# Row numbers and edge weights read from PSUM on VectorE, gather offsets taken directly, and a rearranged seam, in a two-layer graph kernel

## The chip, the cores and the metric

The kernel runs as one program on one NeuronCore of a Trainium2 chip. The metric is the device time of that core in microseconds (us). Before the change it is 3225.76 us, the median of three runs (3219.61 to 3226.62). The engines are called PE (TensorE), PEld (its weight loads), DVE (VectorE), ACT (ScalarE), POOL (GpSimd) and SP (SyncE).

## The reference, cut to what matters

The input is a graph of N = 6250 nodes with 128 features and E = 106,250 edges, sorted by destination. Two attention layers follow each other; both sum over the edges that end in a node:

```python
# layer 0, 8 heads of 16
q_dst = Q[dst] + rel_q[edge_type]
k_src = K[src] + rel_k[edge_type] + time_emb @ Wt + bt
v_src = V[src] + rel_v[edge_type]
logits = alpha * sum(q_dst * k_src) / 4 * decay + (1 - alpha) * hyp(m[src], m[dst]) * decay
ex = exp(logits - segment_max(logits, dst)[dst])
attn = ex / segment_sum(ex, dst)[dst]
agg = segment_sum(v_src * attn, dst)      # then Wo, residual, layer norm, FFN, layer norm
# layer 1, 4 heads of 32: the same scheme
logits = sum(leaky_relu(xs[src] + xd[dst] + edge_emb[edge_type]) * att)
agg = segment_sum(xs[src] * softmax(logits over dst), dst)   # then gate, W_out, residual, norms
```

## The kernel before, in words

Nodes are cut into blocks of 120. Edges are worked on in steps of 128; a step lies within one tile of 128 edges and one block, so that a tile with edges of two blocks gives two steps. Four steps make a quad (QS = 4), and there are 221 quads. The program's stages run behind each other: `front` (schedule, projections and tables), `edges0` (the first pass over all edges), `join_tiles` and `nodes0`, `edges1` (the second pass), `join_tiles` and `nodes1`.

Both passes have the same plan. Each engine runs its own list, written out by hand in a function `emit(None, c)` that is called for one iteration c after the other; semaphores tie the lists together. For each quad:

- POOL issues four indirect DMAs (`gather`, L1087 and L1823), which bring 128 rows each from a table in DRAM into a ring in SBUF, `rows`. The ring holds 12 quads in the first pass (RQ0) and 16 in the second (RQ). The row numbers that steer a gather, its offsets, are copied by ACT from a large index tensor into a small tile `idx` ahead of time (`index`, L1217 and L1927), and POOL waits for that copy once in a group. Before a slot is used again, POOL waits for `sums` of the quad that had it.
- `node`, one node number for each edge, comes by DMA from SP. From it a transposed one-hot `oht` is made: on DVE in the first pass (`transposed_onehot`, L1110) and with two ACT instructions in the second (L1934, L1943).
- PE (`edge`, L1290 and L1997) adds up in PSUM (`p_x`) the gathered rows and, through `oht`, the rows of the destinations.
- DVE makes the logits from that, in the first pass by L1146 (plus time features), L1151 (times the queries) and L1156 (sum by head), in the second by L1860, L1869 and L1879.
- After a group of quads (LQ0 = 4 in the first pass, LQ = 8 in the second) comes the seam: PE transposes the group's logits into PSUM (`p_l`), DVE takes running maxima over each node's edges with two scans, ACT takes the exponential, PE transposes back into PSUM (`p_e`), and ACT copies the weights beside the gathered rows (L1243, L1957; semaphore `spread`).
- Some quads later (LAG0 = 7 and LAG = 10) the same quad is summed. DVE builds the one-hot `oh`, 128x(4x122), by comparing the row numbers 0 to 121 (`k.iota`) with `k.code` (L1164, L1865), and multiplies the gathered values with the weights that lie beside them (L1180, L1876; `scaled`). PE multiplies `oh` with the weighted rows into `p_r` (L1320, L2033; `sums`), ACT evicts `p_r` to `bound`, and DVE adds its four steps to the accumulator (`add`, L1135 and L1889).

The block that a step belongs to is known only on the chip. DVE reads it into registers with `load_steps` and uses it as the address of the accumulator, sixteen steps at a time:

```python
if live(i, a) and (a % 4 == 3 or a == 0):
    count["blocks"] = load_steps(nc, k, ET.DVE, 1, nth0(i, a, QS), 4 if a % 4 == 3 else 3)
```

In the first pass this is the first thing in DVE's iteration (L1125), ahead of L1146 and behind a wait for the last add of the iteration before. In the second it stands behind L1879 (L1891).

The second pass starts behind `nodes0` and a clearing of semaphores. There SP loads the index tensor `index1` (L1794), ACT copies the first offsets (L1932), and DVE zeroes the two accumulators with memsets of 120x7128 (L1846) and scales the attention row (L1848).

Of the kernel before, what the change touches and what calls it, by code (L numbers as in the profile page):

```python
# [26 lines left out]
P = 128  # L27
# [99 lines left out]
class Kept:  # L127


    def __init__(self, nc, ctx, io, sz):  # L130
# [29 lines left out]
        self.pair = sb("pair", [P, RQ0 * QS * R0])  # L160
        self.tops = sb("tops", [P, S // (LQ0 * QS), 2])
# [799 lines left out]
def edges0(nc, k):  # L961
# [7 lines left out]
    with ExitStack() as ctx:  # L969
# [7 lines left out]
        idx = [sb(f"idx{u}", [P, GS], I32) for u in range(3)]  # L977
# [17 lines left out]
        p_l, p_e = p_le[:, 0:P], p_le[:, 2 * P:3 * P]  # L995

        weights_in, ready, idx_in = sem("weights_in"), sem("ready"), sem("idx_in")
# [9 lines left out]
        vec = sem("vec")  # L1007
# [16 lines left out]
        with nc.Block() as block:  # L1024
# [78 lines left out]
            def _(dve):  # L1103
                V = nc.vector
                v = Chain(dve, vec)
                V.memset(wbd[:, :, :], 0.0).then_inc(ready, 1)
                v.did(V.memset(acc, 0.0))
# [12 lines left out]
                def emit(i, c):  # L1120
# [4 lines left out]
                    if live(i, a) and (a % 4 == 3 or a == 0):  # L1125
                        count["blocks"] = load_steps(nc, k, ET.DVE, 1, nth0(i, a, QS), 4 if a % 4 == 3 else 3)

                    def add(t):
# [4 lines left out]
                        to = acc[:, bass.ds(count["blocks"][((a - 3) % 4 if a >= 3 else a) * QS + t], 1), :]  # L1133
# [36 lines left out]
                    if maxing:  # L1170
                        u = m1 // LQ0 % 3
                        dve.wait_ge(turned, group(i, m1, 1, 1))
                        dve.wait_ge(group_in[u], slot(i, m1, RQ0, 16 * 2))
                        v.did(V.tensor_tensor(scaled_l[:, :], p_l, decay[u][:, :], ALU.mult))
                    if live(i, w):
                        if w % LQ0 == 0:
                            dve.wait_ge(spread, group(i, w, 1, 1))
                        r = w % RQ0 * QS
# [21 lines left out]
                    if live(i, a):  # L1200
                        dve.wait_ge(vec, count["added"])
                        dve.sem_inc(added, 1)
# [1294 lines left out]
```

## Time and profile before

| | before |
|---|---|
| median of three runs | 3225.76 us (3219.61 to 3226.62) |
| the profiled execution, its own time | 3207.44 us |
| its span, first to last instruction | 3205.6 us |
| mean granted TensorE clock | 0.889 of full speed |
| PE busy | 2423.5 us (76%) |
| DVE busy | 2361.2 us (74%) |
| POOL busy | 1935.5 us (60%) |
| ACT busy | 1398.0 us (44%) |

The profile shows one execution with every instruction's start and duration. "Busy" leaves out waits, register work and DMA issues on all engines but POOL, whose indirect DMAs count as its work. A group is all instructions of one line, operation and shape; behind the bar stand their busy time, the mean of one, and the idle time of the engine just before them with what ended it. "Issue" is idle time that no wait of the profile explains. The first gather of the first pass starts at 315.75 us, that of the second at 1876.48.

### The profile page before, as it was taken

How to read it: one execution, taken by the hardware profiler on the slowest of the kernel's cores; microseconds unless marked ns; L12 is line 12 of the kernel's file. 1: busy time of each engine (PE TensorE's matmuls, PEld its weight loads, DVE VectorE, ACT ScalarE, POOL GpSimd, SP SyncE). 2: the span in 40 equal slices, each digit the busy share in tenths (PEclk: the TensorE clock that was granted, in tenths of full speed). 3: DMA queues.
4: the chain of work that ended last, by engine and by line, in shares of the span. 5: the costliest groups of instructions: out<-in, count | busy, mean ns of one | idle time of the engine just before them, and what ended most of it. 6: DMA issues, size and time to landing. Idle time of an engine off the chain costs nothing. (4 is left out here: it accounts for less than half of the span.)

```text
span 3205.6 us, 48812 instructions
## 1 busy us (share of the span) xinstructions
PE 2423.5 (76%) x11946; PEld 1882.5 (59%) x11946; DVE 2361.2 (74%) x5743; ACT 1398.0 (44%) x4327; POOL 1935.5 (60%) x1957
## 2 busy tenths in 40 slices
PE   4887789888888888887578846767677677666744
PEld 3565566666666666666333435666666666666633
DVE  7444798988898888988656646667666766666767
ACT  2433355555555555554155533333333333333306
POOL 1000777777777777774600047777777777777464
PEclk8898899999999999998799978888888888888865
DMA  5376766666666666673200133333333333333131
GB/s 112 58 208 199 209 196 196 195 193 194 195 194 194 191 192 195 194 194 98 67 16 25 32 89 72 79 83 83 82 83 83 82 83 83 82 82 82 36 61 41
DMA packets 253628, 387.14 MB, mean 121 GB/s; under 512 B 70853, under 2 KB 168881, under 8 KB 249642
## 3 DMA queue, kind: packets, MB, share of 16 engines
q0 software_dynamic: 86432, 239.62, 28.7%
q1 hardware_dynamic: 132662, 130.96, 16.1%
q10 hardware_dynamic: 34260, 13.43, 1.7%
q8 instruction: 107, 1.75, 0.2%
q14 instruction: 167, 1.37, 0.1%
HBM read 342.88 MB, written 40.92 MB: 120 GB/s over the span
## 5 line engine op out<-in xcount | busy, mean ns | idle before, releaser
L1831 POOL DMA_INDIRECT pair<-d_table,e_idx x884 | 868.1, 982 | 563.6 <-ACT e_idx L1932 294.6
L1094 POOL DMA_INDIRECT pair<-d_table,e_idx x884 | 899.7, 1018 | 276.6 <-issue 248.2
L2007 PE MATMUL e_p_x<-pair,iden 128*128 128x264 f32 x884 | 343.7, 476 | 318.7 <-issue 250.2
L1308 PE MATMUL e_p_x<-big,e_oht 128*128 x1768 | 455.4, 380 | 0.0
L1966 ACT COPY pair<-e_p_r 122x264 f32<-122x264 f32 x442 | 165.5, 375 | 633.8 <-PE e_p_r L2033 632.0
L1860 DVE SCALAR_TENSOR_TENSOR e_prod<-e_p_x,e_att 128x512 f32<-128x512 f32 x221 | 152.9, 692 | 315.0 <-PE e_p_x L2009 302.6
L2007 PEld LDWEIGHTS e_p_x<-pair,iden 128*128 128x128 f32 x884 | 158.6, 223 | 352.6 <-issue 319.2
L1308 PEld LDWEIGHTS e_p_x<-big,e_oht 128*128 128x128 f32 x1768 | 337.4, 191 | 46.4
L2009 PEld LDWEIGHTS e_p_x<-big,e_oht 128*128 128x128 f32 x1768 | 335.3, 234 | 46.5
L1298 PE MATMUL e_p_t<-e_wbd,e_feat 128*128 128x512 f32 x442 | 243.6, 633 | 144.6 <-DVE pair L1146 117.5
L2009 PE MATMUL e_p_x<-big,e_oht 128*128 x1768 | 335.1, 322 | 0.0
L1260 ACT ACTIVATE e_p_x<-e_p_x 128x128 f32<-128x128 f32 x884 | 234.2, 265 | 179.3 <-DVE pair L1151 178.7
L2033 PE MATMUL e_p_r<-pair,e_oh 128*122 128x132 f32 x1768 | 270.1, 301 | 52.3 <-DVE pair L1876 49.2
L2033 PEld LDWEIGHTS e_p_r<-pair,e_oh 128*122 128x122 f32 x1768 | 246.2, 208 | 68.4 <-DVE pair L1876 67.5
L1135 DVE TENSOR_TENSOR big<-big,e_bound 120x136 f32 x884 | 257.2, 291 | 22.7 <-DVE e_lg L1183 15.0
L1306 PE MATMUL e_p_x<-pair,iden 128*128 128x256 f32 x884 | 264.3, 381 | 0.0
L1320 PE MATMUL e_p_r<-pair,e_oh 128*122 128x136 f32 x1768 | 252.7, 287 | 7.5 <-DVE pair L1180 7.5
L1320 PEld LDWEIGHTS e_p_r<-pair,e_oh 128*122 128x122 f32 x1768 | 228.0, 189 | 28.6 <-DVE pair L1180 21.5
L1306 PEld LDWEIGHTS e_p_x<-pair,iden 128*128 128x128 f32 x884 | 168.8, 191 | 118.4 <-issue 106.8
L1889 DVE TENSOR_TENSOR big<-big,pair 120x132 f32 x884 | 210.7, 291 | 30.0 <-issue 18.7
L1252 ACT COPY e_bound<-e_p_r 122x272 f32<-122x272 f32 x442 | 164.6, 385 | 140.2 <-PE e_p_r L1320 83.0
L1146 DVE TENSOR_TENSOR pair<-pair,e_p_t 128x512 f32<-128x512 f32 x221 | 151.5, 685 | 97.6 <-issue 72.6
(362 smaller groups left out, 4223.7 us busy)
## 6 DMA issues: line engine op xcount, KB each, us to landing
pair<-d_table,e_idx POOLq DMA_INDIRECT x1768, 3.5
e_node<-d_node SPq DMA_DIRECT2D x28, 960.0 KB
e_node<-d_node SPq DMA_DIRECT2D x111, 240.0 KB
d_table<-tab_kmv SPq DMA_DIRECT2D x54, 360.0 KB, 3.5
e_feat<-in_edge_attr ACTq DMA_DIRECT2D x442, 16.0 KB
e_feat<-in_edge_attr SPq DMA_DIRECT2D x442, 16.0 KB
e_gate<-d_gate SPq DMA_DIRECT2D x84, 64.5 KB
d_decay<-pair SPq DMA_DIRECT2D x7, 512.0 KB, 4.5
```

The costliest lines, as they stand in the source:

```text
L1094: nc.gpsimd.indirect_dma_start(rows[:, c % RQ0 * QS + t, 0:3 * D], None, k.d_table0, bass.IndirectOffsetOnAxis(ap=idx[c // LQ0 % 3][:, c % ...
L1135: v.did(V.tensor_tensor(to, to, bound[a // BQ % 3][0:BN, a % BQ * QS + t, :].unsqueeze(1), ALU.add))
L1260: last = A.activation(p_x[c % 2][:, t, D:2 * D], p_x[c % 2][:, t, D:2 * D], ACT.Square, accum_out=d2[c // LQ0 % 3][:, c % LQ0 * QS + t:c % ...
L1298: M(p_t[:, :, :].rearrange("p t d -> p (t d)"), feat[c % 6][:, :], wbd[:, :, :].rearrange("p t d -> p (t d)"), start=True, stop=True).then ...
L1306: M(x[:, 2 * h:2 * h + 2, D:2 * D], k.iden[:, :], rows[:, r + 2 * h:r + 2 * h + 2, D:2 * D], start=True, stop=True)
L1308: last = M(x[:, t, :], oht[c % 3][:, t * P:(t + 1) * P], qm[:, bass.ds(of[t], 1), :], start=False, stop=True, skip_group_check=True)
L1320: last = M(p_r[h][0:R_LAST + 1, t - 2 * h, 0:W], oh[w % 2][:, t, :], rows[:, w % RQ0 * QS + t, 2 * D:R0], start=True, stop=True)
L1831: nc.gpsimd.indirect_dma_start(rows[:, r, :], None, k.d_table1, bass.IndirectOffsetOnAxis(ap=idx[c // LQ % 2][:, c % LQ * QS + t:c % LQ * ...
L1889: v.did(V.tensor_tensor(to, to, bound[a // 4 % 2][0:BN, a % 4 * QS + t, :].unsqueeze(1), ALU.add))
L2007: M(x[:, 2 * h:2 * h + 2, 0:W], k.iden[:, :], rows[:, r + 2 * h:r + 2 * h + 2, :], start=True, stop=False)
L2009: last = M(x[:, t, 0:W], oht[c % 4][:, t * P:(t + 1) * P], xd[:, bass.ds(held["blocks"][(c - 1) % 4 * QS + t if c else t], 1), :], start=F ...
L2033: last = M(p_r[h][0:R_LAST + 1, t - 2 * h, 0:W], oh[w % 2][:, t, :], rows[:, w % RQ * QS + t, :], start=True, stop=True)
```

## The change

- Both passes: the row numbers 0 to 121 are copied once into a free part of a PSUM bank (`p_iota`), and the build of `oh` reads them there. The weights for the multiplication are read from the transposed exponentials in PSUM (`p_e`) instead of from beside the rows. The copy of the weights beside the rows, which the sums need, is made by DVE instead of ACT.
- Since PE writes transposes into the bank that DVE reads, DVE waits for the transposes (`turned`, `back`) before it builds `oh`; PE issues them behind its wait for `scaled`, and in the second pass the first transpose of a seam ahead of `edge(c + 1)`.
- The gathers take their offsets straight from `index0` and `index1`; the `idx` tiles, ACT's copies and POOL's waits for them are gone. `index1` lies at the end of `pair` and is loaded by SP at the start of `nodes0`.
- First pass: DVE loads four block numbers in each quad, behind the build of `oh`, for the quad after. Two small vectors (`unpart`, `ones`) are made and not used; the transposed one-hots stay on DVE.
- Second pass: the accumulators are zeroed by two ACT instructions behind its first one-hots; DVE's first iteration waits for them.

```diff
@@ Kept
+        self.index1 = self.pair[:, RQ0 * QS * R0 - S:RQ0 * QS * R0].bitcast(I32)
@@ edges0
-        p_l, p_e = p_le[:, 0:P], p_le[:, 2 * P:3 * P]
+        p_l, p_iota = p_le[:, 0:P], p_le[:, P:P + R_LAST + 1]
+        p_e = p_le[:, 2 * P:3 * P]
...
-                    if c % LQ0 == 0:
-                        pl.wait_ge(idx_in, group(i, c, 1, 1))
...
-                            bass.IndirectOffsetOnAxis(ap=idx[c // LQ0 % 3][:, c % LQ0 * QS + t:c % LQ0 * QS + t + 1], axis=0))\
+                            bass.IndirectOffsetOnAxis(ap=k.index0[:, c * QS + t:c * QS + t + 1], axis=0))\
...
+                v(V.tensor_copy(p_iota, k.iota[:, 0:R_LAST + 1]))
...
-                    if live(i, a) and (a % 4 == 3 or a == 0):
-                        count["blocks"] = load_steps(nc, k, ET.DVE, 1, nth0(i, a, QS), 4 if a % 4 == 3 else 3)
...
-                        to = acc[:, bass.ds(count["blocks"][((a - 3) % 4 if a >= 3 else a) * QS + t], 1), :]
+                        to = acc[:, bass.ds(count["blocks"][t], 1), :]
...
+                    if maxing:
+                        dve.wait_ge(turned, group(i, m1, 1, 1))
                     if live(i, w):
+                        if w % LQ0 == 0:
+                            dve.wait_ge(back, group(i, w, 1, 1))
                         if i is not None or w >= 2:
                             dve.wait_ge(sums, nth0(i, w - 1, 2))
-                        V.tensor_tensor(oh[w % 2][:, :, :], bc(k.iota[:, 0:R_LAST + 1], 1, QS),
+                        V.tensor_tensor(oh[w % 2][:, :, :], bc(p_iota, 1, QS),
                                         bc(k.code[:, bass.ds(nth0(i, w, QS), QS)], 2, R_LAST + 1), ALU.is_equal)
+                    if live(i, a + 1):
+                        upcoming = load_steps(nc, k, ET.DVE, 1, nth0(i, a + 1, QS), 1)
...
-                            dve.wait_ge(spread, group(i, w, 1, 1))
-                        r = w % RQ0 * QS
+                            V.tensor_copy(rows[:, r:r + GS, 3 * D:R0], p_e.rearrange("p (h t) -> p t h", h=H0)).then_inc(spread, 1)
...
-                        V.tensor_tensor(val, val, bc(rows[:, r:r + QS, 3 * D:R0], 3, D // H0), ALU.mult).then_inc(scaled, 1)
+                        share = p_e.rearrange("p (h t) -> p t h", h=H0)[:, w % LQ0 * QS:w % LQ0 * QS + QS, :]
+                        V.tensor_tensor(val, val, bc(share, 3, D // H0), ALU.mult).then_inc(scaled, 1)
...
-                    if c % LQ0 == 3 and live(i, m1):
-                        act.wait_ge(back, group(i, m1, 1, 1))
-                        r = m1 % RQ0 * QS
-                        A.copy(rows[:, r:r + GS, 3 * D:R0], p_e.rearrange("p (h t) -> p t h", h=H0)).then_inc(spread, 1)
...
                         pe.wait_ge(scaled, nth0(i, w + 1))
+                    if c % LQ0 == 1 and live(i, c - 1 - LQ0):
+                        g = c - 1 - LQ0
+                        pe.wait_ge(leveled, group(i, g, 1, 1))
+                        nc.tensor.transpose(p_l, lg[g // LQ0 % 3][:, :, :].rearrange("p h t -> p (h t)"), k.iden[:, :])\
+                            .then_inc(turned, 1)
+                    if c % LQ0 == 3 and live(i, c - 3 - LQ0):
+                        g = c - 3 - LQ0
+                        pe.wait_ge(exps, group(i, g, 1, 1))
+                        nc.tensor.transpose(p_e, ext[:, :], k.iden[:, :]).then_inc(back, 1)
+                    if live(i, w):
+                        if w % LQ0 == 0:
+                            pe.wait_ge(spread, group(i, w, 1, 1))
...
-                    if c % LQ0 == 0 and live(i, c - LQ0):
...
-                    if c % LQ0 == 2 and live(i, c - 2 - LQ0):
...
@@ nodes0
+                sp.dma_start(k.index1, k.d_index1).then_inc(index_in, 16)
                 sp.wait_ge(folded, 1)
@@ edges1
-                sp.dma_start(index1[:, :], k.d_index1).then_inc(index_in, 16)
...
-                for u in range(2):
-                    v.did(V.memset(k.acc1[u], 0.0))
+                v(V.tensor_copy(p_iota, k.iota[:, 0:R_LAST + 1]))
...
+                    if maxing:
+                        dve.wait_ge(turned, m // LQ + 1 if i is None else i * 2 + (m // LQ + 1))
...
-                        V.tensor_tensor(oh[w % 2][:, :, :], bc(k.iota[:, 0:R_LAST + 1], 1, QS),
+                        V.tensor_tensor(oh[w % 2][:, :, :], bc(p_iota, 1, QS),
...
-                            dve.wait_ge(spread, w // LQ + 1 if i is None else i * 2 + (w // LQ + 1))
+                            dve.wait_ge(back, w // LQ + 1 if i is None else i * 2 + (w // LQ + 1))
...
+                dve.wait_ge(zeroed, 2)
                 whole(emit)
...
-                act.wait_ge(index_in, 16)
-                index(None, 0)
                 act.wait_ge(signs, 2)
                 for c in range(3):
                     distance(None, c)
                     transposed_onehot(None, c)
+                for u in range(2):
+                    A.activation(k.acc1[u], k.part[0:BN, 0:1].unsqueeze(2).broadcast_to([BN, NBP, W]), ACT.Copy, scale=0.0)\
+                        .then_inc(zeroed, 1)
...
-                    if live(i, c + 1):
-                        edge(i, c + 1)
                     if c % LQ == 0 and live(i, m):
                         pe.wait_ge(x_read, nth(i, m + LQ) if live(i, m + LQ - 1) else sz.quads)
                         nc.tensor.transpose(p_l[:, :], lg[m // LQ % 2][:, :, :].rearrange("p h t -> p (h t)"), k.iden[:, :])\
                             .then_inc(turned, 1)
+                    if live(i, c + 1):
+                        edge(i, c + 1)
+                    if live(i, w):
+                        pe.wait_ge(scaled, nth(i, w + 1))
```

## Rows read from the trace of the kernel before

**Rows 1.** Windows of both passes: us, busy us (x) by engine, PEclk, DMA share, GB/s.
```profile
400.00:1440.00 1040.00, 929.81 (x4421) 714.11 (x4420) 934.00 (x2260) 558.21 (x2307) 800.83 (x785) 1.00 0.69 194
1960.00:2980.00 1020.00, 718.81 (x4036) 632.41 (x4036) 711.86 (x1872) 399.93 (x900) 777.13 (x798) 0.84 0.37 82
```

**Rows 2.** The page's groups: POOL's gathers of both passes.
```profile
L1831 POOL DMA_INDIRECT pair<-d_table,e_idx x884 | 868.1, 982 | 563.6 <-ACT e_idx L1932 294.6
L1094 POOL DMA_INDIRECT pair<-d_table,e_idx x884 | 899.7, 1018 | 276.6 <-issue 248.2
```

**Rows 3.** Timeline, first pass, POOL: start, us, engine, line, operation [idle before].
```profile
601.44 1.70 POOL L1094 DMA_INDIRECT pair<-d_table,e_idx  x1 [0.30 <-issue]
603.45 0.95 POOL L1094 DMA_INDIRECT pair<-d_table,e_idx  x1 [0.30 <-issue]
...
622.58 1.70 POOL L1094 DMA_INDIRECT pair<-d_table,e_idx  x1 [0.30 <-issue]
```

**Rows 4.** The same stretch on DVE.
```profile
600.85 0.66 DVE L1164 TENSOR_TENSOR e_oh<-iota_f,code 128x488 f32<-128x488 f32 x1
601.42 0.69 DVE L1180 TENSOR_TENSOR pair<-pair 128x512 f32<-128x512 f32 x1
602.02 0.30 DVE L1135 TENSOR_TENSOR big<-big,e_bound 120x136 f32 x1
```

**Rows 5.** DVE's waits: us in total, times, longest.
```profile
DVE e_prod L1860 <- PE e_p_x L2009: 302.6, 109, 8.8
DVE pair L1146 <- issue: 72.6, 54, 1.4
...
DVE pair L1146 <- DVE big L1135: 24.3, 105, 0.6
```

**Rows 6.** DVE's groups by form: busy us, mean ns, idle us before.
```profile
L1135 DVE TENSOR_TENSOR big<-big,e_bound 120x136 f32 x884 | 257.2, 291 | 22.7 <-DVE e_lg L1183 15.0 <-DVE big L1135 4.8 <-issue 2.9
...
L1180 DVE TENSOR_TENSOR pair<-pair 128x512 f32<-128x512 f32 x221 | 150.3, 680 | 0.0
L1151 DVE TENSOR_TENSOR pair<-pair,e_p_x 128x512 f32<-128x512 f32 x221 | 150.3, 680 | 7.8 <-PE e_p_x L1308 7.7
...
L1174 DVE TENSOR_TENSOR e_scaled_l<-e_p_le,e_decay 128x128 f32<-128x128 f32 x56 | 15.8, 282 | 0.0
```

**Rows 7.** Timeline, second pass, DVE, at a load of sixteen block numbers.
```profile
2282.01 0.17 DVE L1879 TENSOR_TENSOR e_lg<-e_lg,e_p_x 128x16 f32<-128x16 f32 x1
2282.88 0.95 DVE L1889 TENSOR_TENSOR big<-big,pair 120x132 f32 x4 [0.69 <-issue]
```

**Rows 8.** Timeline of all engines, the second pass's start.
```profile
1872.16 0.34 SPq L1794 DMA_DIRECT2D pair<-d_index  x1
...
1875.44 0.22 ACT L1932 COPY e_idx<-pair 128x32 int32<-128x32 int32 x1 [7.04 <-DMA pair<-d_index]
...
1876.48 1.04 POOL L1831 DMA_INDIRECT pair<-d_table,e_idx  x1 [294.58 <-ACT e_idx L1932]
...
1880.32 7.80 POOL L1831 DMA_INDIRECT pair<-d_table,e_idx  x1 [0.31 <-issue]
...
1883.90 0.72 ACT L1941 ACTIVATE e_oht<-e_node,e_unpart 128x512 f32<-128x512 bf16 x1 [8.25 <-DMA e_node<-d_type]
...
1887.15 0.16 DVE L1848 TENSOR_SCALAR e_att<-e_att 128x128 f32<-128x128 f32 x1
```

**Rows 9.** Timeline, second pass, DVE and POOL.
```profile
2218.45 0.94 POOL L1831 DMA_INDIRECT pair<-d_table,e_idx  x1 [0.30 <-issue]
...
2218.84 0.69 DVE L1860 SCALAR_TENSOR_TENSOR e_prod<-e_p_x,e_att 128x512 f32<-128x512 f32 x1 [7.35 <-PE e_p_x L2009]
...
2219.45 0.66 DVE L1865 TENSOR_TENSOR e_oh<-iota_f,code 128x488 f32<-128x488 f32 x1
...
2219.70 1.22 POOL L1831 DMA_INDIRECT pair<-d_table,e_idx  x1 [0.31 <-issue]
...
2222.39 0.69 DVE L1860 SCALAR_TENSOR_TENSOR e_prod<-e_p_x,e_att 128x512 f32<-128x512 f32 x1
```

More of the change, by code:

```diff
@@ L1105, in _ @@
                 v = Chain(dve, vec)
+                V.tensor_scalar(unpart[:, :], k.part[:, :], -1.0, None, ALU.mult).then_inc(signs, 1)
+                V.memset(ones[:, :], 1.0).then_inc(signs, 1)
                 V.memset(wbd[:, :, :], 0.0).then_inc(ready, 1)
+                v(V.tensor_copy(p_iota, k.iota[:, 0:R_LAST + 1]))
                 v.did(V.memset(acc, 0.0))
@@ L1202, in emit @@
                         dve.sem_inc(added, 1)
+                    if live(i, a + 1):
+                        count["blocks"] = upcoming
                     count["base"] += v.n
@@ L1215, in _ @@
                 A = nc.scalar
-                def index(i, c):
-                    if i is not None or c >= 3 * LQ0:
-                        b = c - 2 * LQ0 - 1
-                        act.wait_ge(rows_in[b % RQ0], slot(i, b, RQ0, 16 * QS))
-                    A.copy(idx[c // LQ0 % 3][:, :], k.index0[:, bass.ds(nth0(i, c, QS), GS)]).then_inc(idx_in, 1)
                 tiles = {}
@@ L1236, in emit @@
                 def emit(i, c):
[L1237 to L1243 removed]
+                    w = c - LAG0 - 1
                     if live(i, w):
@@ L1276, in emit @@
                         A.copy(k.tops[:, bass.ds(group(i, g), 1), :], top[g // LQ0 % 2][:, 0:P:P - 1].unsqueeze(1)).then_inc(kept, 1)
-                for g in range(2):
-                    index(None, g * LQ0)
                 for c in range(5):
@@ L1755, in edges1 @@
         att = sb("att", [P, D])
-        idx = [sb(f"idx{u}", [P, LQ * QS], I32) for u in range(2)]
         oht = [sb(f"oht{u}", [P, QS * P]) for u in range(4)]
@@ L1861, in emit @@
                                                      ALU.max, ALU.mult))
+                    m = c - LQ
+                    maxing = c % LQ == 0 and live(i, m)
+                    if maxing:
+                        dve.wait_ge(turned, m // LQ + 1 if i is None else i * 2 + (m // LQ + 1))
                     if live(i, w):
@@ L1892, in emit @@
                         counted["blocks"] = load_steps(nc, k, ET.DVE, 1, nth(i, a, QS), 4 if a else 1)
-                    m = c - LQ
-                    maxing = c % LQ == 0 and live(i, m)
                     if maxing:
@@ L1925, in _ @@
                 A = nc.scalar
-                def index(i, c):
-                    u = c // LQ % 2
-                    if i is not None or c >= 2 * LQ:
-                        b = c - LQ - 1
-                        act.wait_ge(rows_in[b % RQ], 16 * QS * (b // RQ + 1) if i is None else i * (16 * QS) + 16 * QS * (b // RQ + 1))
-                    A.copy(idx[u][:, :], index1[:, bass.ds(nth(i, c, QS), LQ * QS)]).then_inc(idx_in, 1)
                 def distance(i, c):
@@ L1950, in emit @@
                         distance(i, c + 3)
-                    if c % LQ == 2 and live(i, c - 2 + LQ):
-                        index(i, c - 2 + LQ)
-                    if c % LQ == 1 and live(i, c - 1 - LQ):
-                        m = c - 1 - LQ
-                        act.wait_ge(back, m // LQ + 1 if i is None else i * 2 + (m // LQ + 1))
-                        r0 = m % RQ * QS
-                        A.copy(rows[:, r0:r0 + LQ * QS, D:W], p_e[:, :].rearrange("p (h t) -> p t h", h=H1)).then_inc(spread, 1)
                     if live(i, w):
```

50 lines of the change are left out of this document (20 added, 30 removed).

## The prediction

> **What bounds the kernel now.** I read the busy time of the two gather passes, then POOL's groups, then POOL and DVE side by side in a few microseconds of each pass, then DVE's waits. In both passes POOL is busy for 77% of the time and no engine for 100% [rows 1], but the 884 gathers of a pass stand a constant 0.3 us apart (idle 276.6 us in the first pass, 248.2 of it issue, so 0.31 for each) [rows 2]: POOL never rests longer than it takes to issue the next one. An undisturbed gather takes 0.945 us (rows of 0.94 and 0.95) [rows 3, 9], so a pass can't be shorter on POOL than 884 x (0.945 + 0.303) = 1103 us, 5.0 us for a quad of four gathers. The means are higher, 1.018 and 0.982 us [rows 2]: 899.7 - 884 x 0.945 = 64 us too long in the first pass, 868.1 - 835.4 = 33 us in the second.
>
> What lengthens them is seen side by side. The gather at 601.44 takes 1.70 us and ends at 603.14; on DVE L1164, L1180 and L1135 follow each other without a gap until 602.32, and each of them reads two SBUF operands [rows 3, 4]. The gather's end lies 0.82 us behind theirs. At 2219.70 a gather of the second pass takes 1.22 us and ends at 2220.92, 0.81 us behind the end of the one-hot build L1865 (2220.11), though L1869, with one SBUF operand, runs on from there [rows 9]. So a gather stops near its start until the two-operand instruction that DVE is in has ended, and runs its last 0.82 us after it.
>
> The passes have different bounds. In the first, the long gather returns after 622.58 - 601.44 = 21.14 us [rows 3], which is four quads. DVE waits for no other engine there: its one large idle entry is issue, 54 x 1.35 us ahead of L1146, the sixteen block numbers that are loaded once in four quads while the engine stands still; ahead of that instruction it loses 0.23 us in other quads (24.3 us in 105) [rows 5]. POOL could do four quads in 16 x 1.248 = 19.97 us, and the collisions hold it at just DVE's 21.14: whenever it gains, its next read falls into one of DVE's pairs. So in the first pass DVE is the bound, and POOL's 64 us are mostly slack made visible. In the second pass DVE waits 302.6 us for L2009's sums [rows 5], and it does a quad in 2222.39 - 2218.84 = 3.55 us where its rows are there [rows 9]; POOL alone is the bound, and its 33 us count.
>
> **The change, part by part.** My sum is made against the profiled execution, 3207.44 us (span 3205.6). It is 18.3 below the median of the three timed runs, 3225.76; I subtract the gain from the median.
>
> *Block numbers in the first pass.* Four are loaded in every quad, behind the dispatch of L1164's build, instead of sixteen in every fourth quad with the engine idle. Sixteen cost 1.35 - 0.23 = 1.12 us beyond the usual gap, so four cost 0.28 if the price goes by number and up to 1.12 if each call pays it all. The build alone covers 0.66 us [rows 4], and the add ahead of it 0.29 [rows 6]. That loads run while DVE works is seen in the second pass: of the same sixteen, issued behind L1879, 0.69 us stays visible ahead of L1889 [rows 7]. I take nothing for the new loads, so the gain is 1.12 us in a group; without cover four loads would cost 1.1 to 4.5.
>
> *The weights' copy moves from ACT to DVE*: 128x128 out of PSUM, once in four quads (56) and once in eight (28). DVE has no such copy; L1174 reads the same tile with another in 0.28 us [rows 6], of which some 0.08 overlaps its neighbours (L1180 begins 0.09 before L1164 ends [rows 4]). I take 0.2, between 0 and 0.28. In the second pass DVE's spare 1.4 us of a quad (5.0 - 3.55) hides it.
>
> *One-hot and weight multiplication read one operand from PSUM.* For the instruction itself: L1151 with a PSUM operand takes 680 ns, L1180 with both in SBUF 680 [rows 6]; I take 0. The Trainium skill (VectorE: DVE Perf Modes, the section on the TRN2 errata) gives a PSUM source 62 cycles more of fixed cost than an SBUF one. By that, an estimate from that page, the eight instructions of a group would lose about 0.5 us, 27 us in 53 groups, and the sum below would be 46 us; L1151 and L1180 do not show it.
>
> For the gathers: of DVE's two-operand instructions the adds (four of 0.29 us in a quad [rows 6]), scans and a few small ones stay. First pass: DVE's group becomes 21.14 - 1.12 + 0.2 = 20.2 us, POOL's floor is 19.97, so the two are nearly even. If reads fell anywhere, each would meet an add with 16 x 0.291 / 20.2 = 23% and then wait 0.15, 0.54 us in a group, with the scans some 0.75: POOL at 20.7. If it locks to DVE as now, 20.2. I take 20.3, nearer the row that shows locking. Eight quads at the start carry less work, so 213 / 4 = 53 groups x 0.84 = 44 us, and two loads fewer in the tail, 2 us. Bounds: 53 x (21.14 - 20.0) = 60 and 53 x (21.14 - 20.7) = 23.
>
> Second pass: 33 us is 6.9 in one gather at its start (7.80 - 0.945 [rows 8]) and 26 in the rest. In one span of eight quads (2206 to 2246) eight gathers are long, by 0.99 us in all; three of them (0.28, 0.28, 0.16; two are like the first of [rows 9]) end behind L1865, so 0.7 of it goes by the change. That leaves 8 of the 26; the phases will shift, so I take 10: gain 16. Bounds: 3 left (gain 23), or adds met at random, 884 x 4 x 0.291^2 / 2 / 5.0 = 30 (loss 4).
>
> *Early index and zeroing at the second pass's seam.* POOL's first gather waits for the index load (SP, 1872.16) and ACT's copy (1875.44) and starts at 1876.48; the fourth sits until DVE's scaling of the attention row ends at 1887.31, 0.81 before its own end [rows 8]. Without index wait and without DVE's zeroing ahead of that scaling, POOL starts near 1872.7 (half a microsecond behind SP's first issue): 3.8 + 6.9 = 10.7 us. ACT now zeroes 2 x 7128 columns behind its first one-hots; it did 512 in 0.72 us [rows 8], so at most 20 us, and DVE starts up to that later. POOL runs 16 quads (80 us) ahead before it needs DVE, and DVE gains 1.4 us a quad, so I take 0; uncovered it would be some 12.
>
> *The rest.* New waits of DVE for the two transposes stand ahead of L1164's and L1865's builds. Queued behind them are weight multiplication and adds, for which PE's sums wait. PE issues these transposes right after the edge sums that DVE's own multiplication, over 2 us earlier in the quad (L1151, L1156, L1117 and an add), has already waited for; in the second pass the first transpose moves ahead of the edge sums. Nothing, at worst 0.3 in a group. PE itself did 929.81 us in 1040 [rows 1], 4.72 in a quad of 5.28, still under 5.05. ACT loses the index and weight copies: no gain, it is not late. Two small vectors and one PSUM copy at the first pass's start, the index load on SP in the node stage: under 1 us.
>
> Sum: 46 + 16 + 10.7 = 73 us. 3225.8 - 73 = **3153 us** (3134 on the profiled scale).
>
> **Rivals.** *POOL at random phases* (20%): first pass 20.7 a group, 23 + 2; second 10.7 - 4: 32 us, 3194. For it: POOL's floor is within 0.3 of DVE's new group. Against: 64 us now where many more collisions are possible. *POOL entirely clear* (8%): 62 + 23 + 11 = 96 us, 3130.
>
> *PSUM reads don't free the gather* (7%): another pause ends with those rows by chance. Then POOL keeps 21.1 us a group, only the seam gains: 11 us, 3215. The Trainium skill (SBUF — State Buffer, "Who interferes with whom") points this way in one clause: tensor_tensor takes only the read side of the shared ports while descriptors need the write side; another clause says that two SBUF inputs do hold up a reading GpSimd. The 1.70 and 1.22 us gathers agree with the second.
>
> *Reading PSUM so is dearer* (5%, the slower side): the weights are read 16 elements apart, each repeated; no DVE row shows that pattern. It would sit in the first pass's 8 instructions of a group, 426 in all: from 73 / 426 = 0.17 us each it decides, and at 0.25 it gives 3225.8 - 73 + 107 = 3260. Against: L1151.
>
> **How the numbers follow.** The forecast has 60%. Range 3126 to 3197: forecast, random phases and clear POOL, 88% less their edges. 0.2% (6.5 us) is about what can be told from no change. Faster: 0.60 + 0.20 + 0.08 and half of the third rival, 0.91; same 0.04; slower 0.05.
>
> **What would show it.** Right: ahead of L1146 no issue gap of 1.35 us; the repeat of four quads near 20.3 us; no gather of 1.70 us; POOL's second-pass gathers at 0.955 us in the mean, the first of them within 1 us of the stage's first DMA issue; L1164, L1180 and L1865 within 10 ns of now. Wrong: POOL's mean unchanged with builds from PSUM, or the repeat above 20.8 us, or a new idle entry of DVE for the transposes.

## The result, and the profile after

The changed kernel takes 3122.95 us (median; 3116.77 to 3128.77). The kernel before, run beside it, takes 3222.69 (3212.06 to 3226.62): a ratio of 0.9695, 95% interval 0.9664 to 0.9726. A later comparison gave 0.9721 (0.970 to 0.9741) with 3127.97 us. Three executions in the comparisons further down, of 3651.14, 5757.89 and 5758.44 us, are slow ones and are left out of every median given here. The forecast of 3153 us had the direction and put the gain in the right places, but was short on the size; 3122.95 lies 3 us below its range.

The profiled execution takes 3128.77 us (span 3127.0), 78.7 us less than that of before. In the text a *pass* is the time from the start of POOL's first gather to the end of its last, and its *excess* is the sum of its 884 gather durations less 884 x 0.945 us:

| | first pass, excess | second pass, excess |
|---|---|---|
| before | 1168.9, 64 us | 1137.1, 33 us |
| before, another execution | 1175.6, 71 us | 1135.6, 31 us |
| after | 1112.7, 8 us | 1110.3, 6 us |
| after, another execution | 1112.5, 8 us | 1109.6, 5 us |

So 56 us come from the first pass, 27 from the second and 3.6 from ahead of the second's first gather. The stretch from the last gather of the first pass to SP's first issue of the second is 6 us longer after in this pair (393 against 388 us) and 1 us shorter in the second pair. Over all runs of this document it goes from 384 to 400 us, so I count it as spread.

POOL's two groups on the page after, which answer [rows 2]:

```profile
L1826 POOL DMA_INDIRECT pair<-d_table,pair x884 | 841.1, 951 | 566.2 <-POOLq L204 297.0
L1094 POOL DMA_INDIRECT pair<-d_table,index x884 | 843.5, 954 | 276.3 <-issue 253.6
```

The idle time is as before, so still 0.3 us for each gather; the means fell from 982 and 1018 ns to 951 and 954, and both passes now stand within 10 us of POOL's floor of 1103. The windows of both passes after [rows 1] show what gained by it: DVE is busy for 95% of the first pass, before it was 90%.

```profile
400.00:1400.00 1000.00, 934.09 (x4472) 715.73 (x4471) 950.03 (x2335) 541.70 (x2233) 757.94 (x795) 1.00 0.73 204
1900.00:2900.00 1000.00, 707.16 (x4030) 628.75 (x4029) 714.13 (x1890) 390.44 (x847) 757.28 (x797) 0.86 0.38 83
```

DVE's waits after, against [rows 5]. Of the 72.6 us of issue ahead of L1146 0.2 us are left; the third line is new, the wait for ACT's zeroing at the second pass's start:

```profile
DVE e_prod L1854 <- PE e_p_x L1995: 262.7, 109, 8.0
...
DVE pair L1146 <- DVE big L1135: 35.0, 158, 0.6
...
DVE e_prod L1854 <- ACT big L1974: 21.6, 1, 21.6
```

DVE's groups by form after, against [rows 6]: weight multiplication (L1877, L1186) and one-hot build (L1863, L1168) with a PSUM operand take what they took from SBUF (680 ns in [rows 6]; the builds of before are the first two lines). The new waits for the transposes cost 2.9 us in all, ahead of L1863.

```profile
L1865 DVE TENSOR_TENSOR e_oh<-iota_f,code 128x488 f32<-128x488 f32 x221 | 145.3, 657 | 1.3
L1164 DVE TENSOR_TENSOR e_oh<-iota_f,code 128x488 f32<-128x488 f32 x221 | 145.0, 656 | 0.0
...
L1877 DVE TENSOR_TENSOR pair<-pair,e_p_e 128x512 f32<-128x512 f32 x221 | 149.6, 677 | 0.0
L1186 DVE TENSOR_TENSOR pair<-pair,e_p_le 128x512 f32<-128x512 f32 x221 | 149.3, 676 | 0.0
L1863 DVE TENSOR_TENSOR e_oh<-e_p_l,code 128x488 f32<-128x488 f32 x221 | 145.1, 657 | 4.4 <-PE e_p_l L2003 2.9 <-PE e_p_r L2020 0.3
L1168 DVE TENSOR_TENSOR e_oh<-e_p_le,code 128x488 f32<-128x488 f32 x221 | 145.0, 656 | 0.2 <-issue 0.2
...
L1183 DVE COPY pair<-e_p_le 128x128 f32<-128x128 f32 x56 | 15.4, 276 | 0.0
```

The first pass in the timeline, POOL and then DVE, as in [rows 3, 4]. A slightly long gather returns after 802.51 - 782.42 = 20.09 us, four quads. It ends 0.81 us behind L1120 (782.12 + 0.48), the transposed one-hot, and not behind a pair of L1164 and L1180 as before. The gather at 793.74 starts inside the multiplication L1186 (793.51 to 794.18), which now reads PSUM, and takes its usual 0.94.

```profile
782.42 0.99 POOL L1094 DMA_INDIRECT pair<-d_table,index  x1 [0.30 <-issue]
783.72 0.94 POOL L1094 DMA_INDIRECT pair<-d_table,index  x1 [0.30 <-issue]
...
793.74 0.94 POOL L1094 DMA_INDIRECT pair<-d_table,index  x1 [0.30 <-issue]
...
802.51 1.00 POOL L1094 DMA_INDIRECT pair<-d_table,index  x1 [0.30 <-issue]
```

```profile
782.12 0.48 DVE L1120 TENSOR_SCALAR e_oht<-e_node,part 128x512 f32<-128x512 bf16 x1
...
793.31 0.27 DVE L1183 COPY pair<-e_p_le 128x128 f32<-128x128 f32 x1
793.51 0.67 DVE L1186 TENSOR_TENSOR pair<-pair,e_p_le 128x512 f32<-128x512 f32 x1
...
802.22 0.48 DVE L1120 TENSOR_SCALAR e_oht<-e_node,part 128x512 f32<-128x512 bf16 x1
```

The second pass's start, as in [rows 8]: POOL's first gather stands 0.74 us behind SP's first issue (4.32 before), and DVE's first work waits for ACT's zeroing until 1848.39.

```profile
1822.23 0.35 SPq L1792 DMA_DIRECT2D e_att<-in_L_gnn_att  x1
...
1822.97 1.04 POOL L1826 DMA_INDIRECT pair<-d_table,pair  x1 [296.96 <-POOLq L204]
...
1848.39 0.69 DVE L1854 SCALAR_TENSOR_TENSOR e_prod<-e_p_x,e_att 128x512 f32<-128x512 f32 x1 [21.64 <-ACT big L1974]
```

### The profile page after: what moved, and what is told of

Same layout as the page of the kernel before. It is cut to its first block and busy times, and to the rows that moved or that the text cites. A ratio compares the mean times of both kernels' runs of the same rounds, so it can differ in the third digit from the quotient of the medians.

```text
span 3127.0 us, 48874 instructions
## 1 busy us (share of the span) xinstructions
PE 2414.5 (77%) x11946; PEld 1876.9 (60%) x11946; DVE 2361.8 (76%) x5829; ACT 1376.4 (44%) x4161; POOL 1853.1 (59%) x1957
## 5 line engine op out<-in xcount | busy, mean ns | idle before, releaser
L1826 POOL DMA_INDIRECT pair<-d_table,pair x884 | 841.1, 951 | 566.2 <-POOLq L204 297.0
L1094 POOL DMA_INDIRECT pair<-d_table,index x884 | 843.5, 954 | 276.3 <-issue 253.6
L1993 PE MATMUL e_p_x<-pair,iden 128*128 128x264 f32 x884 | 335.4, 466 | 308.7 <-issue 236.0
L1302 PE MATMUL e_p_x<-big,e_oht 128*128 x1768 | 454.5, 380 | 0.0
L1302 PEld LDWEIGHTS e_p_x<-big,e_oht 128*128 128x128 f32 x1768 | 336.8, 191 | 46.1
L1995 PEld LDWEIGHTS e_p_x<-big,e_oht 128*128 128x128 f32 x1768 | 326.5, 229 | 44.5
L1995 PE MATMUL e_p_x<-big,e_oht 128*128 x1768 | 327.0, 316 | 0.0
L2020 PE MATMUL e_p_r<-pair,e_oh 128*122 128x132 f32 x1768 | 276.7, 306 | 16.5 <-DVE pair L1877 15.2
L2020 PEld LDWEIGHTS e_p_r<-pair,e_oh 128*122 128x122 f32 x1768 | 255.5, 214 | 25.2 <-DVE pair L1877 24.5
L1326 PEld LDWEIGHTS e_p_r<-pair,e_oh 128*122 128x122 f32 x1768 | 226.8, 191 | 32.6 <-DVE pair L1186 28.6
L1933 ACT ACTIVATE e_oht<-e_node,e_unpart 128x512 f32<-128x512 bf16 x221 | 160.5, 726 | 41.9 <-ACT pair L1951 16.3
```

What stands on the lines that cost most here:

```text
L1094: nc.gpsimd.indirect_dma_start(rows[:, c % RQ0 * QS + t, 0:3 * D], None, k.d_table0, bass.IndirectOffsetOnAxis(ap=k.index0[:, c * QS + t:c ...
L1302: last = M(x[:, t, :], oht[c % 3][:, t * P:(t + 1) * P], qm[:, bass.ds(of[t], 1), :], start=False, stop=True, skip_group_check=True)
L1326: last = M(p_r[h][0:R_LAST + 1, t - 2 * h, 0:W], oh[w % 2][:, t, :], rows[:, w % RQ0 * QS + t, 2 * D:R0], start=True, stop=True)
L1826: nc.gpsimd.indirect_dma_start(rows[:, r, :], None, k.d_table1, bass.IndirectOffsetOnAxis(ap=index1[:, c * QS + t:c * QS + t + 1], axis=0))\
L1993: M(x[:, 2 * h:2 * h + 2, 0:W], k.iden[:, :], rows[:, r + 2 * h:r + 2 * h + 2, :], start=True, stop=False)
L1995: last = M(x[:, t, 0:W], oht[c % 4][:, t * P:(t + 1) * P], xd[:, bass.ds(held["blocks"][(c - 1) % 4 * QS + t if c else t], 1), :], start=F ...
```

## The experiments

**Both kernels once more**, for the spread of a profiled execution; their passes stand in the table above.

> The kernel before, unchanged, profiled a second time, since its profiled execution (3207 us) was the fastest of its runs. Theory L: in the first pass collisions of POOL's gathers with DVE settle to DVE's own pace, so four quads repeat at 21.1 us again and the total is within 0.3% of 3207 to 3227, with what differs spread over stages. Rival V: the executions differ in how gathers and DVE lock, so the repeat of four quads or the second pass's mean gather (0.982 us) differs by several per cent from the first profile.

> The changed kernel, unchanged, profiled and timed a second time, with the kernel before on the same chip. Theory L: four quads of the first pass at 20.1 us and second-pass gathers at 0.951 us in the mean as in its first profile, and a gain over before between 79 us (the two first profiles) and 100 us (the two medians). Rival V: another lock, with the repeat above 20.3 us or the mean gather above 0.96.

Before: 3213.66 us profiled; after: 3128.57 profiled, median 3127.97. Both theories L hold: four quads of the first pass (mean of quads 40 to 200) take 21.27 us before, 21.19 in the first profile, and 20.14 after in both; the second pass's gathers take 0.980 and 0.951 us. The gain is 84.5 us between the medians of this comparison (3212.45 before) and 85.1 between these profiled executions. Between two executions of one kernel the first pass differs by up to 7 us before and by 0.2 after.

**Block numbers alone.** The kernel before, with four block numbers loaded in each quad behind the one-hot build, no PSUM operands:

```diff
-                    if live(i, a) and (a % 4 == 3 or a == 0):
-                        count["blocks"] = load_steps(nc, k, ET.DVE, 1, nth0(i, a, QS), 4 if a % 4 == 3 else 3)
...
+                    if live(i, a + 1):
+                        upcoming = load_steps(nc, k, ET.DVE, 1, nth0(i, a + 1, QS), 1)
```

> The kernel before with one part of the change: in the first pass four block numbers are loaded in every quad behind the build of the one-hot, instead of sixteen in every fourth quad ahead of L1146. Theory D (DVE sets the pace of the first pass, POOL's long gathers only follow it): the 1.35 us issue gap goes, DVE could repeat at 20.0 us; POOL's floor is 19.97 and with two-operand builds and multiplications still in SBUF it meets more collisions than with the full change, so 20.0 to 20.6 us a group, 25 to 58 us less in all, second pass unchanged. Rival P (the collisions set the pace): the repeat stays at 21.1 us and the total within 5 us of before.

Slower by 0.7%: 3240.27 us in the median, ratio 1.007 (1.0047 to 1.0093). In the profiled execution, the slowest of five (3224.95 to 3256.34), the first pass takes 1203.8 us with 99 us of excess. DVE's gap is gone, and POOL's gathers became longer (page of this kernel, first pass, 1018 ns before):

```profile
L1094 POOL DMA_INDIRECT pair<-d_table,e_idx x884 | 934.4, 1057 | 276.7 <-issue 262.9
```

In DVE's waits of this kernel the gap has turned into a wait for PE's sums of rows that come late:

```profile
DVE pair L1148 <- PE e_p_x L1309: 98.9, 80, 3.8
```

Neither theory had this: D wanted 25 to 58 us less, P the same time. POOL's gathers are held for 35 us more than before, and POOL has become the bound. I take it that the 64 us before were slack only as long as DVE stood still for 1.35 us in each group; why the gathers are held for longer without that gap was not tested.

**PSUM operands alone in the first pass.** The kernel after, with sixteen block numbers again loaded ahead of L1146:

```diff
+                    if live(i, a) and (a % 4 == 3 or a == 0):
+                        count["blocks"] = load_steps(nc, k, ET.DVE, 1, nth0(i, a, QS), 4 if a % 4 == 3 else 3)
...
-                    if live(i, a + 1):
-                        upcoming = load_steps(nc, k, ET.DVE, 1, nth0(i, a + 1, QS), 1)
```

> The changed kernel with the block numbers of the first pass loaded sixteen at a time again, ahead of L1146. Theory D: the first pass repeats at 21.2 us (21.1 and the copy's 0.2, less what DVE's one-hot no longer loses to POOL), no gain there, and the second pass keeps its gain of 37 us with its start: 25 to 40 us less than before. Rival P: the first pass gains as in the whole change (20.1 to 20.4 us a group, some 45 us), 70 to 90 us less than before.

3186.11 us, ratio 0.9913 (0.9899 to 0.9927), 26.3 us less than before, as theory D has it. The first pass takes 1167.0 us, as long as before, with 19 us of excess instead of 64. POOL now waits openly, for the sums that free the ring (POOL's waits of this kernel):

```profile
POOL pair L1094 <- PE e_p_r L1324: 44.4, 85, 0.9
```

That shows DVE as the bound of the first pass before: 45 us of longer gathers became 44 us of waiting. The second pass has its full gain (1109.9). In the first pass, then, against the two executions of before, the operands by themselves shorten it by 2 to 9 us, the loads by themselves lengthen it by 28 to 35, and both together shorten it by 56 to 63.

**Which of the two operands.** The kernel after, first with the row numbers of the one-hot read from SBUF in both passes, then with the weights instead (the edits of the first pass; those of the second are alike):

```diff
-                        V.tensor_tensor(oh[w % 2][:, :, :], bc(p_iota, 1, QS),
+                        V.tensor_tensor(oh[w % 2][:, :, :], bc(k.iota[:, 0:R_LAST + 1], 1, QS),
```

> The kernel after, but the one-hot build of both passes reads its row numbers from SBUF again; the weight multiplication stays on PSUM. Same instructions on every engine, one operand apart. Theory D (a gather is held until a DVE instruction with two SBUF operands ends): the second pass loses what ended behind L1865 before, 15 of 26 us, so it goes from 1109.6 to 1120 to 1130 us; in the first pass a build of 0.66 us in each quad meets a gather at random for 0.66 x 0.66 / 2 / 1.25 = 0.17 us, 0.7 us in a group of four quads, with the adds 1.2 us: POOL at 21.2 against DVE's 20.1, 1125 to 1165 us instead of 1112.5. Median 3150 to 3200 against 3128. Rival B (only the build and the multiplication in one unbroken stretch hold a gather, 1.3 us and more; one alone lets it pass): both passes within 5 us of the kernel after, median 3125 to 3140. Rival N (operands don't matter, the moved waits and loads made the gain): no change at all, 3128.

```diff
+                            dve.wait_ge(spread, group(i, w, 1, 1))
-                        V.tensor_tensor(val, val, bc(share, 3, D // H0), ALU.mult).then_inc(scaled, 1)
+                        V.tensor_tensor(val, val, bc(rows[:, r:r + QS, 3 * D:R0], 3, D // H0), ALU.mult).then_inc(scaled, 1)
```

> The kernel after, but the weight multiplication of both passes reads the weights from SBUF, beside the rows, behind DVE's own copy; the one-hot build stays on PSUM. Theory D: the second pass loses what ended behind L1876 before, 4.2 us of 26, so 1112 to 1118 us instead of 1109.6; the first pass some 10 to 50 us as with the build alone, since the multiplication lasts as long (0.68 us), 1120 to 1165 us. Median 3140 to 3185 against 3128. Rival B (only both in one stretch hold a gather): both passes within 5 us, median 3125 to 3140. Rival W (the 16-apart read of the weights in PSUM costs or saves something of its own): the multiplication's mean differs from 676 ns by over 30 ns.

One-hot from SBUF: 3134.95 us, ratio to before 0.9779 (0.976 to 0.9797), against 0.9721 after. Weights from SBUF: 3195.04 us, 0.9964 (0.9946 to 0.9982). The pages' groups, first of the one, then of the other:

```profile
L1826 POOL DMA_INDIRECT pair<-d_table,pair x884 | 855.6, 968 | 566.3 <-POOLq L204 297.2
L1094 POOL DMA_INDIRECT pair<-d_table,index x884 | 845.1, 956 | 276.5 <-issue 254.1
```

```profile
L1827 POOL DMA_INDIRECT pair<-d_table,pair x884 | 855.8, 968 | 561.1 <-POOLq L204 292.0
L1094 POOL DMA_INDIRECT pair<-d_table,index x884 | 901.4, 1020 | 276.1 <-issue 259.0
```

In the second pass each operand costs 14 to 15 us (1124.7 and 1124.9 us) against 1110: there theory D holds, for the multiplication with more than its 4.2 us. In the first pass the build costs 1.4 us (1114.1) and the multiplication 58 (1170.4, excess 66), though they last 0.66 and 0.69 us. So theory D's numbers miss: the first pass lies below its range with the build and above it with the multiplication, and so do both medians. Its sum for meetings at random fails. The median with the build lies in rival B's range, but the second pass (15 us) and the multiplication refute B; W fails (the multiplication takes 686 ns from SBUF, 676 from PSUM), and N with them. Of the 66 us with the weights from SBUF, 24 are in 115 gathers that end behind the multiplication L1187, and 19 in 21 gathers of up to 1.90 us that end behind L1190, where L1175, L1187 and L1190, each with two SBUF operands, follow each other without a gap. Most of the others end behind adds and L1120. Two gathers that end 0.82 and 0.83 us behind L1187, in this timeline of POOL and DVE, the first at 681.46 + 1.28 against 681.23 + 0.69:

```profile
681.46 1.28 POOL L1094 DMA_INDIRECT pair<-d_table,index  x1 [0.30 <-issue]
...
686.96 1.08 POOL L1094 DMA_INDIRECT pair<-d_table,index  x1 [0.30 <-issue]
```

```profile
681.23 0.69 DVE L1187 TENSOR_TENSOR pair<-pair 128x512 f32<-128x512 f32 x1
...
686.53 0.68 DVE L1187 TENSOR_TENSOR pair<-pair 128x512 f32<-128x512 f32 x1
```

**Kind of instruction or place in the quad?** An undisturbed gather of 0.945 us that runs its last 0.82 us after a release can be held 0.125 us behind its start. Of the gathers 100 to 800 of the first pass after, that point lies inside L1186 in 127 cases, with 33 us of the multiplication left to run, and inside the build, but for one gather, only in its first or last 0.1 us, where it overlaps a neighbour. So the phase may decide. In the next kernel the weights come from SBUF, as in the run above, but in the first pass multiplication and build have changed places (the copy of the weights and its wait go with the multiplication, the wait for `sums` with the build):

```diff
@@ first pass, at the place of the build
...
+                        V.tensor_tensor(val, val, bc(rows[:, r:r + QS, 3 * D:R0], 3, D // H0), ALU.mult)
-                        V.tensor_tensor(oh[w % 2][:, :, :], bc(p_iota, 1, QS),
-                                        bc(k.code[:, bass.ds(nth0(i, w, QS), QS)], 2, R_LAST + 1), ALU.is_equal)
@@ first pass, at the place of the multiplication
...
-                        V.tensor_tensor(val, val, bc(share, 3, D // H0), ALU.mult).then_inc(scaled, 1)
+                        V.tensor_tensor(oh[w % 2][:, :, :], bc(p_iota, 1, QS),
+                                        bc(k.code[:, bass.ds(nth0(i, w, QS), QS)], 2, R_LAST + 1), ALU.is_equal).then_inc(scaled, 1)
```

> The kernel of the run before with the weights multiplied from SBUF (3195 us, first pass 1170.4 us on POOL), but in the first pass DVE multiplies where it built the one-hot, and builds where it multiplied; same instructions, same operands, other order within the quad. Theory L (POOL is locked to DVE at one phase; the place of the multiplication is met by gathers there, 168 times in 700 with 58 us left to run in the kernel after, and the place of the build almost never): the first pass comes back to 1112 to 1125 us, median 3135 to 3155, the second pass stays at 1125 us. Rival K (the multiplication is worse for gathers than the build wherever it stands, because it reads and writes the ring of rows or lies 16 apart): the first pass stays above 1150 us, median above 3175.

3156.52 us, ratio 0.9801 (0.978 to 0.9822), 1.5 us above theory L's range. The first pass is back at 1119.4 us with 15 us of excess; the second, with nothing moved, stays at 1127.7. The page of this kernel, first pass, against 1020 ns with the same operands in the other order:

```profile
L1094 POOL DMA_INDIRECT pair<-d_table,index x884 | 850.1, 962 | 276.4 <-issue 253.7
```

Theory L holds, rival K falls: 51 us hang on where the same instruction stands. My count of 168 in its expectation had in it 41 gathers whose point lies in the overlap of the build and the multiplication; the 43 in the overlap ahead of the build were not held when the build read SBUF, so 127 is the better number.

**What held one gather for 7.80 us** [rows 8]. The kernel after without ACT's zeroing, with DVE's memsets back in three places: behind the scaling of the attention row; ahead of it, with the copy into PSUM between; and ahead of it, next to it.

```diff
-                dve.wait_ge(zeroed, 2)
@@ in one of three places among DVE's first instructions; ACT's two zeroing instructions are gone
+                for u in range(2):
+                    v.did(V.memset(k.acc1[u], 0.0))
```

> The kernel after, but DVE zeroes the two accumulators of the second pass by memsets again, now behind the scaling of the attention row instead of ahead of it; ACT's two zeroing instructions and DVE's wait for them are gone. Theory M (a memset of 120x7128 holds the gather that starts ahead of it): one or two gathers of 6 to 8 us near the pass's start, second pass 5 to 14 us longer than 1110, time 3133 to 3142. Rival A (the scaling behind the memsets was what held the gather of 7.80 us before): no gather above 1.5 us there. DVE's first work then starts 10 us earlier than behind ACT's zeroing, which should be worth nothing, since POOL sets the end: 3125 to 3131.

> The kernel after, but DVE zeroes the accumulators by memsets ahead of the scaling of the attention row, as in the kernel before; ACT's zeroing and DVE's wait for it are gone. With the memsets behind the scaling no gather was held. Theory Q (the scaling, queued behind a running memset, holds a gather from the second memset's start until it has run itself): one gather of 6 to 8 us that ends 0.8 us behind the scaling, second pass 1115 to 1118 us. Rival (the gather of 7.80 us came by the chance of the gathers' start against the memsets): no gather above 1.5 us, second pass 1108 to 1111 us.

> As the run with the memsets ahead of the scaling, but with the copy of the row numbers into PSUM ahead of both memsets, so that the scaling of the attention row is the next instruction behind the second memset, as in the kernel before; in that run the copy stood between them and no gather was held. Theory Q (the scaling, next in line while a memset runs, holds a gather that starts meanwhile until it has run itself): one gather of 5 to 8 us that ends 0.8 us behind the scaling, second pass 1114 to 1118 us. Rival (the gather of 7.80 us of the kernel before had another cause): no gather above 1.5 us, second pass 1108 to 1112 us.

3128.86, 3120.72 and 3130.56 us, one run each; second pass 1108.3, 1110.7 and 1114.4. A gather above 1.5 us is there in the third alone, in its timeline of POOL and DVE:

```profile
1826.40 0.94 POOL L1826 DMA_INDIRECT pair<-d_table,pair  x1 [0.30 <-issue]
1827.65 7.95 POOL L1826 DMA_INDIRECT pair<-d_table,pair  x1 [0.30 <-issue]
1835.91 0.94 POOL L1826 DMA_INDIRECT pair<-d_table,pair  x1 [0.30 <-issue]
```

```profile
1821.29 6.00 DVE L1842 MEMSET big<- 120x7128 f32 x1 [1.55 <-issue]
1828.72 6.00 DVE L1842 MEMSET big<- 120x7128 f32 x1 [1.43 <-issue]
1834.63 0.16 DVE L1844 TENSOR_SCALAR e_att<-e_att 128x128 f32<-128x128 f32 x1
```

It ends 0.81 us behind the scaling, like that of before. The gathers from 1821.41 to 1827.34 run beside the first memset and are not held. The second timeline has the copy behind the second memset, and there gathers run beside both memsets:

```profile
1822.11 6.00 DVE L1841 MEMSET big<- 120x7128 f32 x1 [1.44 <-issue]
1828.03 0.27 DVE L1842 COPY e_p_l<-iota_f 128x122 f32<-128x122 f32 x1
1828.33 0.29 DVE L1844 TENSOR_SCALAR e_att<-e_att 128x128 f32<-128x128 f32 x1
```

No gather of that run is longer than 1.04 us near the start. So theory M falls, and rival A holds for the first of the three. Theory Q missed in the second run, where its rival, chance, came out with 1110.7 us; the copy that stood there between memset and scaling had not been reckoned with. The third run has no such copy, and there theory Q holds: a scaling of 0.16 us, next in line behind a memset, holds a gather until it has run. Four profiled executions have that order, both of before, that with the block numbers alone and this one, and each has one such gather, of 7.80, 8.00, 7.86 and 7.95 us. With the last 0.82 us behind the release, the hold began near 1827.8, almost 1 us ahead of the second memset; in the other three it began 0.8 to 1.0 us ahead of it, too. What DVE does in that gap no row shows. So it was the order, and not the move to ACT, that freed this gather. DVE's first work starts 26 us behind SP's first issue with ACT's zeroing and 19 us behind it with DVE's own memsets, and that makes no difference to the pass.

**Index load.** The kernel after with `index1` loaded at the second pass's start, where POOL waits for it:

```diff
-                sp.dma_start(k.index1, k.d_index1).then_inc(index_in, 16)
@@ edges1
+                sp.dma_start(index1, k.d_index1).then_inc(index_in, 16)
...
+                pl.wait_ge(index_in, 16)
```

> The kernel after, but the index tensor is loaded at the start of the second pass, as before, and POOL's first gather waits for that load (no copy of the offsets in between). Theory: the first gather starts 3.0 to 4.0 us after SP's first issue instead of 0.74 us, and the pass's end moves by the same, 2.3 to 3.3 us; time 3128 to 3134. Rival (the load is hidden, because POOL must wait for something else at the stage's start anyway): the first gather starts within 1.5 us of SP's first issue.

3131.27 us, one run. Its timeline has SP's first issue at 1821.22, the index load's at 1821.62, and POOL's first gather 7.30 us behind the first:

```profile
1821.22 0.35 SPq L1790 DMA_DIRECT2D e_att<-in_L_gnn_att  x1
1821.62 0.43 SPq L1791 DMA_DIRECT2D pair<-d_index  x1
```

```profile
1828.52 1.04 POOL L1825 DMA_INDIRECT pair<-d_table,pair  x1 [303.38 <-DMA pair<-d_index]
```

That is 3 to 4 us more than expected (the time lies within its range); the load, second in SP's queue here, took 6.1 us to land. From SP's first issue to the end of the last gather it is 1114.9 us against 1111.1 after, so the early load is worth 3.8 us.

## Why the prediction was short

1. *"I subtract the gain from the median."* This step failed, and it is the largest: the 18.3 us between the profiled execution and the median of before were carried over to the kernel after as if they were fixed. They are spread: the medians of before in the four timed comparisons were 3222.69, 3212.45, 3206.12 and 3218.25 us, the second profiled execution of before lies within 1.2 us of its comparison's median (3213.66 and 3212.45), and the kernel after took 3128.77 us profiled and 3122.95 in the median, the other way round. The gain is 99.7 and 84.5 us between medians, 78.7 and 85.1 between profiled executions. My range had no term for this spread. Of the 30 us between 3153 and 3122.95, 18.3 are this offset, 5.7 the sum (78.7 instead of 73) and 5.8 the distance between the profile and the median after. In the sum the first pass is 10 us better than forecast and the second 4; the 6 us between the passes, which vary, and 2 us at the ends go against it.
2. *First pass, "I take 20.3".* This term was mis-sized. In quads 40 to 200 a group took 21.19 us before and 20.14 after, a gain of 1.05 us, 55 times; I had 0.84, 53 times. The 1.12 for the loads and the 0.2 for the copy held: the quad that has both took 5.64 us before, 5.83 with PSUM operands and the old loads, and 4.73 after, so 0.19 for the copy and 1.10 for the loads. The 0.1 that I added for meetings with adds had no place, because POOL does lock to DVE, as the sentence ahead of it said. Its gathers are longer by 0.15 us in a group, close to the 0.17 that DVE's 20.14 leaves above POOL's floor of 19.97, and of the pass's 8 us 3.9 end behind one place of the group, L1120. The random rival's 20.7 is refuted with it. DVE loses time as well, which the sum put at nothing: its transposed one-hot takes 0.48 us as a rule, but 53 of the 221 in either kernel take 0.55 to 0.69 us. All but a few of these start 0.50 to 0.61 us behind the start of a gather and end 1.2 us behind it. So it seems that the gather holds them, though no run tests that. Over the pass it comes to 11 us before and 7 after, and these 4 us are a part of the 10. After, for example:

```profile
796.24 0.95 POOL L1094 DMA_INDIRECT pair<-d_table,index  x1 [0.30 <-issue]
796.83 0.60 DVE L1120 TENSOR_SCALAR e_oht<-e_node,part 128x512 f32<-128x512 bf16 x1
```

3. *"POOL's 64 us are mostly slack made visible"* was right for the kernel as it stood (PSUM operands alone: 45 us less of it, and no time), but it wasn't free slack: with the gap alone closed, POOL set a pass 28 to 35 us longer. I had priced the two parts of the first pass as if the loads alone brought the 1.12.
4. *Build and multiplication as one cause.* In the first pass the multiplication carries 58 us and the build 1.4; in the second either brings back 14 to 15, both of them some 20. The eight gathers that I had looked at named the build for the second pass.
5. *Second pass, "I take 10"* of excess left: 5.7 were left, so 20 us of gain instead of 16. *Seam*: 3.6 us for the early start and 6.9 for the held gather, forecast 10.7. With 56 us in the first pass and 20 here, the passes came out between the forecast (46 and 16) and the rival of a POOL entirely clear (62 and 23), nearer to that rival in the first.
6. *Costed at nothing, and nothing:* the PSUM operands (676 and 656 ns), the transposes' waits (2.9 us), ACT's zeroing. So the rival of dearer PSUM reads is refuted. The Trainium skill (VectorE: DVE Perf Modes, the section on the TRN2 errata) gives a PSUM source 62 cycles more of fixed cost, by my estimate from that page 0.06 us for each build and multiplication; the rows above show none.
7. The rival that PSUM reads don't free the gather is refuted by the pairs of runs that differ in one operand. The Trainium skill (SBUF — State Buffer, "Who interferes with whom") has it that two SBUF inputs of a DVE instruction hold up a GpSimd that reads; the runs agree. Its clause that `tensor_tensor` takes only the read side of the shared ports, while the writing of descriptors needs the write side, would have left the gathers alone (the section calls it inferred); 1020 against 954 ns in the first pass, with the weights in SBUF or PSUM, contradict that for these gathers.

What stays open: what in DVE holds a gather before the holder runs; why POOL settles at the phase at which L1120 holds it, and so whether another order of DVE's quad would have done without PSUM; and why the loads alone made the gathers longer. The swapped kernel still built its one-hot from PSUM; both from SBUF in the swapped order was not tried.

## What to carry to other kernels

Before a collision is priced by chance, look whether the two engines are locked: if the long instruction returns with the period of the other engine's loop, its place in that loop decides. Here a reordering was worth 51 us of the 58 that the other memory was worth. Two parts of a change that act on two coupled bounds are not to be added up: here, in the first pass, each alone brought little or a loss. And the distance of one profiled execution from a median was spread here, not an offset: it belongs in the range.

## What the runs showed that was not expected

- A held gather ends 0.81 to 0.83 us behind the end of the DVE instruction that held it, in both passes and for holds from 0.05 to 7 us.
- The holder needn't be running: a 0.16 us scaling next in line behind a memset of 6.00 us held a gather for 7.0 us beyond its usual time, while memsets behind the scaling, and memsets with a copy into PSUM between them and the scaling, held none.
- A single-source instruction holds too: that scaling, and the transposed one-hot L1120 (0.48 us). L1120 in turn takes 0.55 to 0.69 us where it starts some 0.55 us behind a gather.
- The same two-operand multiplication cost 58 us or 7 us in the first pass by its place in the quad.
